# An adaLN block with windowed attention and a mixture of experts: the third down quarter of the last body moved behind the last values and the out projection

## What is computed

```python
mod = (silu(c) @ wmod).reshape(2, 6, 1, -1)
sa, ca, ga, sb, cb, gb = mod[:, 0], ..., mod[:, 5]     # ga, gb: kept at 0.25 or more in size
h = layernorm(x) * (1 + ca) + sa
x = x + ga * attention(h)          # q, k, v, masked softmax over 32 keys, out projection
h = layernorm(x) * (1 + cb) + sb
# experts: w = softmax of the two largest of h @ gate_w
hid = gelu(einsum('td,edf->etf', h, w1) + b1)
o = einsum('etf,efd->etd', hid, w2) + b2
y = layernorm(h + o, ln_g, ln_b)   # one norm per expert
x = x + gb * einsum('et,etd->td', w, y)
```

## Time and profile before

| | |
|---|---|
| runs | 245.43, 245.47, 246.61 us; median 245.47 |
| the profiled execution | 245.09 us, span from the first to the last instruction 243.3 us |
| TensorE matmul busy | 226.8 us, 93% of the span |
| VectorE, ScalarE, GpSimd busy | 74%, 64%, 56% |
| mean granted TensorE clock | 0.987 |

### The profile page before, as it was taken

The page is one execution under the profiler, slowest core; times in us unless marked ns, Lnnn a source line. Parts: engine busy times, 40 slices in busy tenths (PEclk is TensorE's granted clock), DMA queues, the critical chain, the costliest instruction groups (busy, mean ns, idle before and its releaser), DMA issues.

```text
span 243.3 us, 7802 instructions
## 1 busy us (share of the span) xinstructions
PE 226.8 (93%) x3069; PEld 198.3 (81%) x3069; DVE 179.3 (74%) x570; ACT 155.5 (64%) x419; POOL 136.1 (56%) x254
## 2 busy tenths in 40 slices
PE   7878899999999999999999999999999999889950
PEld 3555599889988899889988999889988998679950
DVE  2898778776988499777978598759968694663275
ACT  2358439844993869664984599385975498337830
POOL 8166755366814772467625771577336752476175
PEclk9999999999999999999999999999999999999995
DMA  6950000000000000000000000000000000000000
GB/s 188 355 231 3 1 3 3 1 3 4 12 14 3 3 0 22 7 0 4 22 3 3 3 1 24 5 0 3 22 5 0 3 23 4 3 0 6 19 0 23
DMA packets 5652, 6.23 MB, mean 26 GB/s; under 512 B 336, under 2 KB 5104, under 8 KB 5360
## 3 DMA queue, kind: packets, MB, share of 16 engines
q1 hardware_dynamic: 5616, 5.74, 7.4%
HBM read 4.68 MB, written 1.05 MB: 24 GB/s over the span
## 4 chain that ended last, share of the span: by engine, by line
PE 72%; DVE 19%; POOL 5%; issue 2%; ACT 1%; POOLq 0%; ACTq 0%; DVEq 0%
PE z L1020 16%; PE score L991 6%; PE score L982 5%; DVE q_st L595 5%; PE turns L876 5%; PE turns L877 5%; PE turns L878 5%; DVE ypart L665 3%; PE score L1002 3%; PE score L1067 2%; PE z L1042 2%; PE z L1043 2%; PE z L1044 2%; PE turns L922 2%; PE turns L1088 2%
## 5 line engine op out<-in xcount | busy, mean ns | idle before, releaser
L1020 PE MATMUL z<-w,hid 128*128 128x128 f32 x480 | 61.6, 276 | 0.0
L1020 PEld LDWEIGHTS z<-w,hid 128*128 128x128 f32 x480 | 58.8, 191 | 3.1 <-issue 1.0
L489 ACT ACTIVATE hid<-turns,pack_ffn 128x256 f32<-128x256 f32 x96 | 38.6, 518 | 27.2 <-PE turns L878 27.2
L328 POOL TENSOR_TENSOR ypart<-ypart 128x256 f32<-128x256 f32 (+1 forms) x60 | 36.1, 601 | 16.0 <-DVE ypart L665 13.0
L314 POOL TENSOR_SCALAR zvar<-zss 128x4 f32<-128x4 f32 x32 | 8.2, 256 | 60.2 <-DVE zss L651 52.2
L665 DVE SCALAR_TENSOR_TENSOR ypart<-z,zcoef,ln_gG 128x128 f32<-128x128 f32 x120 | 34.1, 340 | 1.8 <-POOL zcoef L319 1.7
L315 POOL TENSOR_TENSOR zrstd<-zvar,mhalf 128x4 f32<-128x4 f32 x32 | 32.2, 1008 | 2.7
L876 PE MATMUL turns<-h_hi,w_hi 128*128 128x256 f32 x96 | 27.8, 290 | 0.2 <-DVE h_lo L733 0.2
L878 PE MATMUL turns<-h_hi,w_lo 128*128 128x256 f32 x96 | 27.0, 281 | 0.0
L877 PE MATMUL turns<-h_lo,w_hi 128*128 128x256 f32 x96 | 27.0, 281 | 0.0
L442 ACT ACTIVATE v_bd<-turns 64x512 f32<-64x512 f32 x16 | 10.1, 632 | 20.6 <-PE turns L938 20.5
(11 more groups left out here) (157 smaller groups left out, 506.0 us busy)
## 6 DMA issues: line engine op xcount, KB each, us to landing
w<-in_w SPq DMA_DIRECT2D x2, 1024.0 KB, 6.8
out_x<-yout SPq DMA_DIRECT2D x8, 128.0 KB, 1.8
x_tokens<-in_x SPq DMA_DIRECT2D x1, 896.0 KB, 6.6
ln_g<-in_ln_g SPq DMA_DIRECT2D x1, 512.0 KB
pack_mod<-in_pack_mod SPq DMA_DIRECT2D x1, 385.0 KB, 3.1
pack_proj<-in_pack_proj SPq DMA_DIRECT2D x1, 193.0 KB, 4.2
pack_att<-in_pack_att SPq DMA_DIRECT2D x1, 130.5 KB, 4.1
x_tokens<-in_x SPq DMA_DIRECT2D x1, 128.0 KB, 3.0
```

What stands on the lines that cost most here:

```text
L328: cf.link(g.tensor_tensor(ypart[:, tt, at:at + n, :], ypart[:, tt, at:at + n, :], ypart[:, tt, at + n:at + 2 * n, :], ALU.add))
L489: last = a.activation(hid[:, e, c, :], up_bank(i, e)[:, c * STEP:(c + 1) * STEP], ACT.Gelu, bias=b1[:, e, c:c + 1])
L1020: last = mm(z_bank(f, q)[:, e * D:(e + 1) * D], hid[:, ee, c, tt * P:(tt + 1) * P], w2[:, ee * CH + c, :], start=False, stop=e == HALF - 1 ...
```

## The change

In TensorE's list, body 7 alone: `down(6, 2, 0)` stands behind `values(7, 3)` instead of in front of it, `down(6, 2, 1)` stands behind `out_proj(7)` instead of in front of it, and the three products of `keep_warm_last(3)` ahead of `out_proj(7)` are gone. In bodies 1 to 6 the order stays as it was, since `ffn and nxt` holds where `ffn and att` did. No other engine's list is touched.

```diff
                 if nxt:
                     proj_k(n)
                     proj_q(n)
-                if ffn and att:
+                if ffn and nxt:
                     down(f, 2, 0)
                 if att:
                     values(i, 3)
+                if i == STEPS - 1:
+                    down(f, 2, 0)
                 if nxt:
                     proj_v(n)
-                if ffn and att:
+                if ffn and nxt:
                     down(f, 2, 1)
-                if i == STEPS - 1:
-                    keep_warm_last(3)
                 if i == 0:
                     keep_warm(3)
                 if att:
                     out_proj(i)
+                if i == STEPS - 1:
+                    down(f, 2, 1)
                 if i == 0:
                     keep_warm(13)
                 if ffn and att:
```

## The result

| | before | after |
|---|---|---|
| median of 15 runs each | 246.61 us (245.42 to 247.11) | 248.21 us (246.67 to 248.48) |
| ratio of the runs | | 1.0066, 95% interval 1.0049 to 1.0083 |
| the profiled execution | 245.09 us, span 243.3 | 248.17 us, span 246.4 |
| mean granted clock | 0.987 | 0.985 |

The change costs 1.6 us, 0.66%. The forecast was 1.75 us over the kernel before, 0.7%, from a fall of the clock. The absolute time was forecast too low: 247.2, in a range up to 247.9, where the median is 248.21.

What follows compares the result with a forecast made beforehand. It took a chain through VectorE and GpSimd to set the pace until the first up product, then TensorE. Terms 0 + 0.1 + 1.65 = 1.75 us on 245.09 gave 246.8; with 0.38 for the median, 247.2, range 245.4 to 247.9.

Steps and rivals of the forecast that it cites:

- Values forward: Body 7, TensorE: values(7, 3) runs about 1.75 us sooner, but the out projection stays at 212.53; gain taken as 0.
- rival C: Faster: the early values bring the out projection forward to 210.9 us, and the end comes at 243.9; chance 0.04.
- First half: First half of the third quarter, down(6, 2, 0), runs some 0.39 us later behind the values; nobody waits, cost 0.
- the pause: TensorE has nothing to issue from 210.2 us until the out projection at 212.53, a pause of 2.3 us.
- Second half behind the out projection: down(6, 2, 1) behind out_proj(7) delays the turn of xn2 by 0 to 0.2 us; 0.1 taken.
- The others who wait: ScalarE's later squares, GpSimd's later coefficients and the store stay covered, by 1.4, 0.6 and 0.5 us among others; cost 0.
- The clock: TensorE's idle of 2.3 us makes its clock fall to half rate; cost 0 to 2.3 us, 1.65 taken.
- B: The forecast, slower: TensorE's clock falls during or just behind its 2.3 us idle; 246.7 to 247.9 us, chance 0.52.
- A: TensorE's clock is kept through its idle, only 0.1 us is lost: 245.2 profiled, 245.6 as a median; chance 0.42.

## Why the prediction was right and where it was wrong

*Values forward, 0.* Right, by its own mechanism: out projection 5.79 and 5.78 us after the scaling of q = 0. The values ended 2.7 us before VectorE took them (209.89 against 212.60); rival C needed the scaling of q = 1 to start sooner, and it kept its distance of 3.40 us.

*First half, 0, and the pause, 2.3 us.* Right: 2.27.

*Second half behind the out projection, 0.1 us.* A tenth too high: the turn comes 0.07 later with the pause filled, and the first up product not at all.

*The others who wait, 0.* Right as to the end. The squares of q = 3 began at 219.67 and ended ahead of the first gelu at 222.29, though with TensorE slow both were late.

*The clock.* Right in kind and size: of the 1.68 us at the turn 0.07 are those of the order, 1.61 are left, and 1.65 were forecast. That the size came so near is partly luck: it was taken from the 3.17 us that seven slow fillers lasted, whose number the program sets; the slow stretch lasted 3.4 us (215.2 to 218.6). The fall didn't come in the pause but 1.3 us after work had begun again, so the out projection itself ran at the full rate. B had 0.52, and 13 of 15 executions lost the time; A was right as a mechanism, in 2 of 15. But the rows under these odds could not carry them. The fall at the end came 2.0 us after the last product in the profile before; in other profiles, whose ends are alike, it came 3.0 us after it (the pause filled), 4.7 (the change) and 5.2 (three fillers). And the idle of 0.96 us that kept the clock (before 13.09) is there again, 0.97 us, in the profile without the fillers, whose program is the same up to body 7: there the clock fell at 15.2. The Trainium skill's rule that only longer pauses bring a fall (TensorE: Matmul & The Clock Gate, section "HAM oscillation — how this bites in real kernels") does not hold for this kernel: 2.27 us brought it in 13 of 15 executions and about 2.05 in 4 of 12.

*The step that failed: from the profiled execution to the median of the runs.* The median of 248.21 lies 0.3 us above the upper bound of 247.9, although the step of the change is as forecast. I put the sum on 245.47, "0.38 above" the profiled 245.09, as if that were one steady distance; over 15 runs it is 1.52, with a median of 246.61. The first three runs were 245.43, 245.47 and 246.61, and I didn't ask why one lay 1.1 us off. They come from two clusters: six of the 15 runs of the kernel before are at 245.42 to 245.51 and nine at 246.60 to 247.11. Two of the first three were of the rarer kind, and the profiled one too. Had I read the third run as a second cluster, the forecast would have been the same 1.75 us on either, 247.2 or 248.4, and the same bounds (0.2 and 2.3 on 246.61) would have ended at 249.1. The lower edge of B's range doesn't follow from the sum either: its least terms give 245.47 + 1.6 = 247.1, not 246.7. What makes the clusters is the clock at the start, shown by the timelines of the start and by the run without start fillers, in which the lower cluster is gone.

## What to carry to other kernels

Before moving work forward on one engine, look at what stands ahead of its consumer in the consumer's own list: here the values were already 1.04 us early, and the change made them earlier still and left TensorE empty while it waited. Work that seems to be in the way of a wait may be what keeps the clock up; count the idle that is left, not the work that is moved. One fall of the clock in one profile says that it can happen, not after how long an idle. When a chain is shortened, the next cover to run out is in the list of an engine that was never late: here GpSimd's sums, which cost first as a place in the queue and then by slowing VectorE beside them.

When a few runs don't agree by more than the effect in question, look for clusters before a median is used as the base.

## What the runs showed of the hardware

TensorE's clock fell after idles that ended before it fell: after 2.27 us of idle it was granted in full for another 1.3 us of dense work and then halved for 3.4 us, fully busy, at a cost of 1.61 us. Whether it falls differs between executions of one program with one idle: 13 of 15 at 2.27 us, 4 of 12 at about 2.05, none of 12 at 1.62. The length of one idle doesn't decide alone: near the start, where the work is thinner, six of the thirteen profiles show one more fall of 3.4 us, at 7.5 (behind idles of 0.65 to 0.69 us and in one of 0.60) or at 15.2 to 16.8 (behind one of 0.96 to 1.22); the kernel before kept the clock behind one of 0.96. In the profile of the change a single fall lies within the work.

VectorE's operations grew long beside GpSimd's sums L328 of two SBUF inputs: the two tensor_scalar of xn2 from 0.60 to 1.27 us, the cast h_hi from 0.29 to 0.32 up to 0.73, the tensor_tensor h_lo from 0.42 to 0.63; beside GpSimd's operations on 4 elements xn2 stayed at 0.60. With the sums moved away the times came back. The Trainium skill (SBUF — State Buffer, section "Who interferes with whom") has VectorE's casts and tensor_scalar in their fast modes, and its operations with two SBUF inputs, share a port with GpSimd, one of them waiting until the other is done. That agrees with these rows in kind; in which mode the operations ran no row shows.
